# Mixture-of-experts rows: weighted on the way and summed in DRAM by accumulating indirect DMAs

## The reference, cut to what matters

```python
x = x + xattn(layernorm(x), ctx, W_q, W_kv, W_out, ln_gamma, ln_beta)     # x: (2, 512, 128)
x = x + ffn(layernorm(x), Wg, bg, W1, b1, W3, b3, W2, b2)

def ffn(x, ...):                                   # 8 experts, D_MODEL = 128, D_FF = 512
    probs = softmax(x @ Wg + bg)
    top_v, top_i = top_k(probs, 2)
    top_v = top_v / (top_v.sum(-1, keepdims=True) + 1e-6)
    combine = einsum('bsk,bske->bse', top_v, one_hot(top_i, 8))
    out = 0
    for e in range(8):
        h = silu(x @ W1[e] + b1[e]) * (x @ W3[e] + b3[e])
        out = out + combine[..., e:e+1] * (h @ W2[e] + b2[e])
    return out
```

## Time and profile before

| what | value |
|---|---|
| time, median of 3 runs | 189.43 us (188.91 to 189.51) |
| the profiled execution: its own time | 188.9 us |
| the profiled execution: span from first to last instruction | 187.2 us |
| TensorE busy, share of span | 77% |
| VectorE busy | 68% |
| ScalarE busy | 40% |
| GpSimd busy | 42% |
| mean granted TensorE clock | 0.916 of full speed |
| expert loop, first to last scatter | 103.87 to 173.44 us |
| from the landing of the last scatter to the end | 175.68 to 187.2 us |

### The profile page before, as it was taken

One profiled execution on the slowest core, in us unless ns is written; L12 is line 12 of the kernel. 1 busy time (PEld: TensorE's weight loads), 2 busy tenths in 40 slices (PEclk: granted clock), 3 DMA queues, 4 the chain that ended last, 5 costly groups with the idle time before them and its releaser, 6 DMA issues.

```text
span 187.2 us, 3063 instructions
## 1 busy us (share of the span) xinstructions
PE 145.0 (77%) x910; PEld 109.1 (58%) x910; DVE 126.7 (68%) x299; ACT 74.6 (40%) x157; POOL 79.4 (42%) x99
## 2 busy tenths in 40 slices
PE   6597978999999986112399998999999999985000
PEld 6476857899988876111135665676666667664000
DVE  0688999889999378878027676666666666672054
ACT  3176568555666431003013432535344444432000
POOL 2651119553567530100772564565656532324200
PEclk9999999999999999755559999999999999999855
DMA  5999992498000303100121110111111100000272
GB/s 157 321 333 349 349 348 86 210 427 369 7 4 0 112 0 88 30 0 2 42 55 29 32 42 28 42 47 42 42 42 46 44 28 14 32 15 28 61 205 84
DMA packets 16952, 19.62 MB, mean 105 GB/s; under 512 B 1837, under 2 KB 13385, under 8 KB 16681
## 3 DMA queue, kind: packets, MB, share of 16 engines
q1 hardware_dynamic: 14628, 15.54, 24.9%
q0 software_dynamic: 1472, 3.02, 5.4%
q10 hardware_dynamic: 837, 0.87, 1.4%
HBM read 16.28 MB, written 3.15 MB: 104 GB/s over the span
## 4 chain that ended last, share of the span: by engine, by line
PE 56%; DVE 19%; DMA 9%; ACT 7%; issue 5%; POOL 1%; ACTq 1%; DVEq 0%; SPq 0%; POOLq 0%
PE psum L1038 21%; PE psum L1057 9%; PE psum L1089 7%; PE psum L1048 4%; DMA early<-in_L_xattn_W_q_dram 4%; PE psum L1076 3%; DVE perm L726 2%; DVE prob L788 2%; PE psum L836 2%; PE psum L838 2%; PE psum L837 2%; DMA y_back<-y_scratch 2%; ACT probT L523 2%; DVE prob L650 2%; DVE xn L829 2%
## 5 line engine op out<-in xcount | busy, mean ns | idle before, releaser
L1038 PE MATMUL psum<-w,probT 128*128 x92 | 46.0, 623 | 1.0 <-ACT probT L559 1.0
L788 DVE TENSOR_TENSOR prob<-psum,early 128x1024 f32<-128x1024 f32 x23 | 28.2, 1224 | 19.6 <-PE psum L1038 18.5
L446 POOL DMA_INDIRECT y_scratch<-xnT,out_row x23 | 22.6, 982 | 34.2 <-DVE xnT L797 34.2
L438 POOL DMA_INDIRECT g_room<-xf_scratch,idx x23 | 22.4, 973 | 19.2 <-DVE idx L771 12.5
L1057 PEld LDWEIGHTS psum<-w,probT 128*128 128x128 f32 x184 | 22.4, 192 | 10.1 <-issue 10.1
L1057 PE MATMUL psum<-w,probT 128*128 x184 | 24.7, 277 | 2.9 <-ACT probT L574 2.9
L415 POOL TENSOR_TENSOR prob<-prob,rowsum 128x1232 f32<-128x1232 f32 x8 | 18.0, 2249 | 17.4 <-DVE rowsum L641 17.3
L1038 PEld LDWEIGHTS psum<-w,probT 128*128 128x128 f32 x92 | 16.4, 199 | 14.6 <-issue 14.6
L569 ACT ACTIVATE prob<-prob 128x512 f32<-128x512 f32 x23 | 14.5, 629 | 25.5 <-DVE prob L788 25.5
L819 DVE TENSOR_TENSOR probT<-prob 128x512 f32<-128x512 f32 x23 | 15.9, 692 | 11.8 <-ACT prob L569 11.8
L1089 PE MATMUL psum<-vo,probT 128*128 128x128 f32 (+1 forms) x160 | 19.5, 277 | 0.3
(11 more groups left out here) (128 smaller groups left out, 203.8 us busy)
## 6 DMA issues: line engine op xcount, KB each, us to landing
w<-in_L_ffn_W_dram SPq DMA_DIRECT2D x24, 256.0 KB, 5.8
early<-in_L_ffn_b_dram SPq DMA_DIRECT2D x2, 2048.0 KB, 10.5
early<-in_L_xattn_W_kv_dram SPq DMA_DIRECT2D x2, 512.0 KB, 7.2
y_back<-y_scratch SPq DMA_DIRECT2D x4, 256.0 KB, 3.7
early<-in_L_xattn_W_q_dram ACTq DMA_DIRECT2D x1, 512.0 KB, 8.0
early<-in_L_xattn_W_out_dram SPq DMA_DIRECT2D x1, 512.0 KB, 9.8
early<-in_L_ffn_b_dram SPq DMA_DIRECT2D x1, 512.0 KB, 13.8
xf_scratch<-xf SPq DMA_DIRECT2D x2, 256.0 KB, 2.6
```

The lines of the kernel that those rows point to most:

```text
L438: pool.indirect_dma_start(xg[:, j % GR, :], None, xf_dram[:, :], bass.IndirectOffsetOnAxis(ap=idx[:, j:j + 1], axis=0)).then_inc(xg_ok[j % ...
L446: pool.indirect_dma_start(y_dram[:, :], bass.IndirectOffsetOnAxis(ap=out_row[:, j:j + 1], axis=0), y_sb[:, j % YR, :], None).then_inc(y_st ...
L788: dve.tensor_tensor(pre[:, j % 3, :, :], psum[:, 2 * (j % 2):2 * (j % 2) + 2, :], b13[:, :, bass.ds(expert[j], 1), :].rearrange("p a e f - ...
L1038: ins = pe.matmul(psum[:, 2 * (j % 2) + a, :], xt[:, j % 2, :], w13[:, bass.ds(expert[j], 1), a, :].rearrange("p e f -> p (e f)"), start=T ...
```

## The change

Nothing of the sorting or of the matmuls changes. These parts do:

1. **Gates earlier, and through DRAM.** `gates` moves from the expert loop into the routing, after the last `one_hots` and before the instructions that end in `eid` and `idx`. Rows of xf_scratch are 129 elements long (XW): the last is the gate of that (token, k). SP waits for the gates and writes them with two DMAs, each of 1024 elements of 4 B, one for each row. The first gather waits for these too.
2. **Weighting in the loop.** The gathered rows bring their gate along as column 128. h is multiplied by it (a scalar_tensor_tensor in place of a tensor_tensor, 128x512), and so is the bias b2 in `bias_down` (the same exchange of kinds, 128x128).
3. **Sum in DRAM.** SP stores x2 group by group into a new DRAM tensor acc_scratch, right behind the two stores of xf of the group; one more store of zeros fills 128 padding rows. `scatter(j)` adds its rows to acc_scratch by an accumulating indirect DMA. A token's two rows come in different tiles, so each scatter waits until the one before it has landed in whole.
4. **End.** No read back and no sums: when the last scatter has landed, SP and ScalarE each issue one copy of 256 KB from acc_scratch to the output, DRAM to DRAM.
5. **Buffers.** The gather ring gets 23 buffers (one for each tile), the result ring goes from 6 to 4 and waits for the landing of scatter j - 4. `out_row` comes from `idx` by two instructions, behind a wait for it; one iota is gone.

```diff
@@ constants @@
+        XW = P + 1
-        gate_w = sb("gate_w", [P, T, K])
+        gate_w = sb("gate_w", [P, K, T])
-        xf_dram = nc.dram_tensor("xf_scratch", [ROWS, P], F32, kind="Internal")
-        y_dram = nc.dram_tensor("y_scratch", [ROWS + NT * P, P], F32, kind="Internal")
-        GR = 16
-        YR = 6
+        xf_dram = nc.dram_tensor("xf_scratch", [ROWS, XW], F32, kind="Internal")
+        acc_dram = nc.dram_tensor("acc_scratch", [N + P, P], F32, kind="Internal")
+        YR = 4
...
@@ sync @@
             sp.dma_start(xf_dram[PAD_ROW:PAD_ROW + P, :], zero_rows[:, :]).then_inc(xf_st, 16)
+            sp.dma_start(acc_dram[N:N + P, :], zero_rows[:, 0:P]).then_inc(acc_init, 16)
...
                 for k in range(K):
                     row = k * (N + P) + g.start * P
-                    sp.dma_start(xf_dram[row:row + len(g) * P, :].rearrange("(t p) d -> p t d", p=P),
+                    sp.dma_start(xf_dram[row:row + len(g) * P, 0:P].rearrange("(t p) d -> p t d", p=P),
                                  xf[:, g.start:g.stop, :]).then_inc(xf_st, 16)
-
-            for s in range(YR):
-                sp.wait_ge(y_st[s], 16 * len(range(s, NT, YR)))
-            for b in range(B):
+                sp.dma_start(acc_dram[g.start * P:g.stop * P, :].rearrange("(t p) d -> p t d", p=P),
+                             x2[:, g.start:g.stop, :]).then_inc(acc_init, 16)
+            sp.wait_ge(gate_ok, 1)
+            with nc.allow_non_contiguous_dma(reason="one gate for each row"):
                 for k in range(K):
-                    row = k * (N + P) + b * BANK
-                    sp.dma_start(y_back[:, k, b * TB:(b + 1) * TB, :],
-                                 y_dram[row:row + BANK, :].rearrange("(t p) d -> p t d", p=P)).then_inc(back[b], 16)
-            out_v = out.rearrange("b (t p) d -> p (b t) d", p=P)
-            for n, tiles in enumerate(OUT_PARTS):
-                sp.wait_ge(o_ok, tiles.stop)
-                sp.dma_start(out_v[:, tiles, :], xn[:, tiles, :]).then_inc(stored, 16)
-            sp.wait_ge(stored, 16 * len(OUT_PARTS))
+                    row = k * (N + P)
+                    sp.dma_start(xf_dram[row:row + N, P:P + 1].rearrange("(t p) d -> p t d", p=P),
+                                 gate_w[:, k, :].rearrange("p (t o) -> p t o", o=1)).then_inc(xf_st, 16)
+
+            sp.wait_ge(acc_st, 16 * NT)
+            out_v = out.rearrange("b n d -> (b n) d")
+            sp.dma_start(out_v[0:BANK, :], acc_dram[0:BANK, :]).then_inc(stored, 16)
+            sp.wait_ge(stored, 32)
...
@@ gpsimd @@
                 if j == 0:
                     pool.wait_ge(idx_ok, 1)
-                    pool.wait_ge(xf_st, 16 * (1 + K * G))
-                elif j >= GR:
-                    pool.wait_ge(xt_mm, j - GR + 1)
-                pool.indirect_dma_start(xg[:, j % GR, :], None, xf_dram[:, :],
-                                        bass.IndirectOffsetOnAxis(ap=idx[:, j:j + 1], axis=0)).then_inc(xg_ok[j % GR], 16)
+                    pool.wait_ge(xf_st, 16 * (1 + K * G + K))
+                pool.indirect_dma_start(xg[:, j, :], None, xf_dram[:, :],
+                                        bass.IndirectOffsetOnAxis(ap=idx[:, j:j + 1], axis=0)).then_inc(xg_ok[j], 16)
...
                 if j == 0:
                     pool.wait_ge(row_ok, 1)
-                pool.indirect_dma_start(y_dram[:, :], bass.IndirectOffsetOnAxis(ap=out_row[:, j:j + 1], axis=0),
-                                        y_sb[:, j % YR, :], None).then_inc(y_st[j % YR], 16)
+                    pool.wait_ge(acc_init, 16 * (1 + G))
+                else:
+                    pool.wait_ge(acc_st, 16 * j)
+                pool.indirect_dma_start(acc_dram[:, :], bass.IndirectOffsetOnAxis(ap=out_row[:, j:j + 1], axis=0),
+                                        y_sb[:, j % YR, :], None, compute_op=ALU.add).then_inc(acc_st, 16)
...
@@ scalar, behind its loop @@
+            act.wait_ge(acc_st, 16 * NT)
+            act.dma_start(out.rearrange("b n d -> (b n) d")[BANK:N, :], acc_dram[BANK:N, :]).then_inc(stored, 16)
...
@@ vector @@
             one_hots(2)
             one_hots(3)
+            gates()
...
             dve.tensor_scalar(idx[:, :], psum[:, IDX_BANK, 0:NT], row_base[:, 0:1], None, ALU.add).then_inc(idx_ok, 1)
-            link(dve.scalar_tensor_tensor(out=unused[:, :], in0=psum[:, IDX_BANK, 0:NT], scalar=0.0, in1=iota_pad[:, :],
-                                          op0=ALU.is_equal, op1=ALU.mult))
-            dve.scalar_tensor_tensor(out=out_row[:, :], in0=psum[:, IDX_BANK, 0:NT], scalar=row_base[:, 0:1], in1=unused[:, :],
-                                     op0=ALU.add, op1=ALU.add).then_inc(row_ok, 1)
+            dve.wait_ge(idx_ok, 1)
+            link(dve.tensor_scalar(second[:, :], idx[:, :], float(N + P), -float(N + P), ALU.is_ge, ALU.mult))
+            dve.tensor_tensor(out_row[:, :], idx[:, :], second[:, :], ALU.add).then_inc(row_ok, 1)
...
                 if j >= YR:
-                    dve.wait_ge(y_st[j % YR], 16 * (j // YR))
-                dve.tensor_tensor(y_sb[:, j % YR, :], psum[:, 7, 0:P],
-                                  b2[:, bass.ds(expert[j], 1), :].rearrange("p e d -> p (e d)"), ALU.add).then_inc(y_ok, 1)
+                    dve.wait_ge(acc_st, 16 * (j - YR + 1))
+                dve.scalar_tensor_tensor(out=y_sb[:, j % YR, :], in0=b2[:, bass.ds(expert[j], 1), :].rearrange("p e d -> p (e d)"),
+                                         scalar=xg[:, j, P:P + 1], in1=psum[:, 7, 0:P], op0=ALU.mult, op1=ALU.add).then_inc(y_ok, 1)
...
-                    dve.tensor_tensor(h[:, j % 2, :], silu[:, j % 2, :], pre[:, j % 3, 1, :], ALU.mult).then_inc(h_ok, 1)
-                if j == 4:
-                    gates()
-
-            for t in range(T):
-                if t % TB == 0:
-                    dve.wait_ge(back[t // TB], 16 * K)
-                dve.scalar_tensor_tensor(out=x2[:, t, :], in0=y_back[:, 0, t, :], scalar=gate_w[:, t, 0:1], in1=x2[:, t, :],
-                                         op0=ALU.mult, op1=ALU.add).then_inc(half_sum, 1)
-                dve.wait_ge(half_sum, t + 1)
-                dve.scalar_tensor_tensor(out=xn[:, t, :], in0=y_back[:, 1, t, :], scalar=gate_w[:, t, 1:2], in1=x2[:, t, :],
-                                         op0=ALU.mult, op1=ALU.add).then_inc(o_ok, 1)
+                    dve.scalar_tensor_tensor(out=h[:, j % 2, :], in0=silu[:, j % 2, :], scalar=xg[:, j, P:P + 1],
+                                             in1=pre[:, j % 3, 1, :], op0=ALU.mult, op1=ALU.mult).then_inc(h_ok, 1)
```

More of the change, by code:

```diff
@@ L127, in build @@
         count_init = sb("count_init", [P, (T + 1) * E], F16)
-        zero_rows = sb("zero_rows", [P, P])
+        zero_rows = sb("zero_rows", [P, XW])
         lower = sb("lower", [P, E, E])
@@ L147, in build @@
         idx = sb("idx", [P, NT], U32)
-        unused = sb("unused", [P, NT])
+        second = sb("second", [P, NT])
         out_row = sb("out_row", [P, NT], U32)
@@ L174, in build @@
         xt = probT_room[:, 4 * FF:4 * FF + 2 * P].rearrange("p (n d) -> p n d", n=2)
-        xg = g_room[:, 0:GR * P].rearrange("p (n d) -> p n d", n=GR)
+        xg = g_room[:, 0:NT * XW].rearrange("p (n d) -> p n d", n=NT)
         y_sb = xnT[:, 0:YR, :]
@@ L218, in build @@
         xf_st = sem("xf_st")
-        xg_ok = [sem(f"xg_ok{n}") for n in range(GR)]
-        y_st = [sem(f"y_st{n}") for n in range(YR)]
+        xg_ok = [sem(f"xg_ok{n}") for n in range(NT)]
+        acc_st = sem("acc_st")
+        acc_init = sem("acc_init")
+        gate_ok = sem("gate_ok")
         xt_mm = sem("xt_mm")
@@ L232, in build @@
         expo_ok = sem("expo_ok")
-        back = [sem(f"back{n}") for n in range(B)]
-        half_sum = sem("half_sum")
-        o_ok = sem("o_ok")
         stored = sem("stored")
@@ L662, in _ @@
             sums(T - 1)
-            dve.wait_ge(const_ok, 14)
+            dve.wait_ge(const_ok, 13)
             dve.wait_ge(ld["router"], 32)
@@ L727, in one_hots, with gates @@
                                           ALU.is_equal, ALU.mult).then_inc(perm_ok, 1)
+            def gates():
+                dve.wait_ge(expo_ok, 1)
+                link(dve.tensor_reduce(zsum[:, :], expo[:, :, :], AX.X, ALU.add))
+                link(dve.tensor_tensor(den[:, :], expo[:, :, 0], expo[:, :, 1], ALU.add))
+                link(dve.scalar_tensor_tensor(out=den[:, :], in0=zsum[:, :], scalar=1e-6, in1=den[:, :], op0=ALU.mult, op1=ALU.add))
+                link(dve.reciprocal(den[:, :], den[:, :]))
+                dve.tensor_tensor(gate_w[:, :, :], expo[:, :, 0:K].rearrange("p t k -> p k t"),
+                                  den[:, :].rearrange("p (o t) -> p o t", o=1).broadcast_to([P, K, T]), ALU.mult).then_inc(gate_ok, 1)
             late_stats(4)
@@ L795, in bias_down @@
                 if j >= YR:
-                    dve.wait_ge(y_st[j % YR], 16 * (j // YR))
-                dve.tensor_tensor(y_sb[:, j % YR, :], psum[:, 7, 0:P],
```

(18 more changed lines are left out.)

5 lines of the change are left out of this document (removed).

## The result

The changed kernel takes 210.49 us (210.13 to 211.01, 4 runs) against 189.4 us (188.91 to 189.51): the ratio is 1.1115, 95% interval 1.1079 to 1.1152. It is 11% slower, where 1.4% faster was forecast. The profiled execution took 210.13 us, its span is 208.4 us, 21.2 longer than before.

What follows compares the result with a forecast made beforehand. The expert loop was taken as bound by TensorE at 3.158 us a tile. Tail -7.7, stall before gather 0 +4.7 and later last landing +0.4 gave -2.6 us, so 186.8 us against the median; range 183.2 to 197.

Steps and rivals of the forecast that it cites:

- The scatters' spacing: Expert loop: waiting for the previous scatter's landing leaves the period unchanged; the last landing comes 0.4 us later.
- L: Accumulating scatter's time from issue to landing: taken as 2.8 us, between 2.3 and 4.8; free in the loop up to 2.89.
- My lower bound: Least time from issue to landing of an accumulating scatter: the plain scatter's 2.3 us.
- The 0.27: Time in us from a semaphore to GpSimd's next scatter issue, added to the landing time for the spacing.
- A: Rival, expert loop: the accumulating scatters take over from TensorE as the bound; 196.5 us at a 3.3 us landing; chance 0.35.
- its sum: Rival's last landing: 103.87 + 4.7 + 22 x (L + 0.27) + L, for L above 2.89.
- The tail: After the last landing: two DRAM copies replace reads back, sums and stores; 3.85 us for 11.52, 7.7 saved.
- Before gather 0: End of routing: gate DMAs delay gather 0 from 88.51 to 93.2, 4.7 us lost (bounds 2.7 and 8.8).
- the row of 512 B pieces: Gate DMAs before the first gather: each 4 B piece priced like a 512 B store piece, 16.7 ns, adding 2.0 us.
- Rival B: Gate writes before the first gather: 4 B pieces dear at 51 ns, stall 8.8 us, total 190.9 us; chance 0.13.
- The loop's other terms: Expert loop: gates leaving return 1.24 us; two VectorE instructions cost some 0.07 us more each, hidden; no further clock loss.
- The read-modify-write rule: Skill rule on scatters: same-row packets overlap in an engine, against serial row cost; landing 2.5 us, forecast 0.9 lower.

Runs made afterwards that it cites:

- Run 1: Changed kernel with the scatter writing plainly instead of adding, every wait kept: 189.0 us, ratio 0.9961 to the kernel before.
- run 6: Changed kernel with scatters adding only 64 of 128 columns, into a tensor of their own: 207.73 us, ratio 1.0922 to the kernel before.
- Run 5: Changed kernel with a scatter's two waits swapped, first the previous landing, then its own result: 201.63 us, ratio 1.0659 to the kernel before.
- run 7: Kernel before with only the gates moved right behind out_row, into VectorE's idle time: 188.82 us, ratio 0.9944.

## Why the prediction was wrong, step by step

**The step that failed is "The scatters' spacing".** It said that a scatter follows the one before by L + 0.27 with L = 2.8, so 3.07, free under 3.16. It measured 3.92 at the end of the loop and 4.18 on average, and TensorE had to follow. Both terms were too small: L, the time from issue to landing, and the wake, the time from the landing to GpSimd's next issue.

- *L* is 3.17 to 3.3 with nothing else in flight and 3.6 in the median, not 2.8. I placed it by the one part that I thought grew, a read in DRAM. More than half of the growth at the end, 0.58 of 0.93, is GpSimd, whose issue goes from 0.97 to 1.55 and in the loop at times to 2.01. Run 1 shows that the add does it, run 6 that it goes by row and not by byte. My lower bound rested on a plain scatter's issue, which the add doesn't keep.
- *The 0.27* was read from a scatter that has one wait. In the changed scatter the landing is waited for second, behind the result, and from the landing to the issue pass 0.73 to 0.77. Run 5 gets 0.43 of it back by the order of the two, 8.9 us in all, more than the whole gain of the tail; run 1 shows the 0.27 with both waits in place, where the result is what comes last. The sum would have been lost on this term alone: 2.8 + 0.74 = 3.54 is over 3.16.

The rival that came true is A, by its mechanism and its place: the spacing is L plus the wake, GpSimd waits for the landing, and TensorE is no longer full, where before it was busy 50.87 of 50.90 us. Busy time from the first to the last scatter:

```profile
108.77:200.69 91.92, 68.89 (x358) 46.06 (x356) 46.21 (x63) 28.76 (x62) 52.53 (x37) 0.91 0.22 27
```

TensorE has 68.89 of 91.92 us. With the measured spacing and landing its sum gives 103.87 + 4.7 + 22 x 4.18 + 3.17 = 203.7 for the last landing, which came at 203.86. But it carried L alone as the unknown, up to 3.3 in the range, and the wake as known. Had it had 0.74, then L = 3.3 would have been 206.8 us, 22 x 0.47 = 10.3 more than 196.5, and L = 2.8 a loss too. The rest up to 210.5 is mostly the longer landings in the middle of the loop: 22 x (4.18 - 3.3 - 0.74) = 3.1.

**The tail** was right: 7.0 saved for 7.7. The two copies land in 3.3 and 3.9 where 3.3 was taken.

**Before gather 0** was right in sum, 4.82 for 4.7, and that is luck: three errors cancel. The chain there:

```profile
89.01 3.42 DMA xf_scratch<-gate_w
92.43 0.02 issue
92.45 0.02 POOLq L430
92.47 0.86 issue
93.33 2.87 DMA g_room<-xf_scratch,idx
```

The second gate DMA lands in 3.42, so by the landing the 120 further pieces of 4 B cost (3.42 - 2.2) / 120 = 10 ns each and not 16.7, which is 0.78 us less than forecast. The Trainium skill (DMA: Bandwidth & Descriptors, Bandwidth) gives about 10.5 ns as the least for a packet; with its figure the term would have been closer than with the row of 512 B pieces. The engines' own records give less. SP's queue from 88 to 93.3 us, where it carries these two DMAs alone:

```profile
q1 hardware_dynamic: 2080, 0.01, 17.9%
```

That is 0.179 x 16 x 5.3 / 2080 = 7.3 ns a packet, so as a least time the 10.5 isn't borne out here.

Against the 0.78, the second DMA is issued 0.31 later than forecast, and 0.90 us pass from the landing to the gather where I had 0.3. I called that a wait for idx alone, but gather 0 has two waits in both kernels, first for idx and then for the stores. In the kernel before idx came last, 0.29 before the issue; now the stores do, and they are waited for second. It is the same error as in the spacing. Rival B fell with this: small pieces are cheap.

**The loop's other terms** held. No clock was lost on top: gather 0 to scatter 0 takes 15.44 for 15.36. The two kinds of VectorE instruction cost 60 ns more each (L817 752 ns for 692, L804 341 for 282) and nothing of it is on the path: in run 1 the scatters 0 to 6 are 3.158 apart, at (127.92 - 108.97) / 6. The gates' 1.24 us do come back, as run 7 shows on the kernel before; in the changed kernel they came back into a loop that no longer waited for TensorE.

**The read-modify-write rule** of the Trainium skill (same page, Two DMAs through the same engine are not ordered) was taken to speak against a serial cost for the rows. The traces don't contradict it: behind GpSimd's issue an accumulate needs 1.62 us and a plain scatter 1.27. The 0.35 more would be 44 ns for each of the eight rows of an engine if they came one after the other; whether they overlap no run shows. GpSimd's own share is the larger one here, and the prediction had none for it.

## What to carry to other kernels

A wait that makes a stream of DMAs serial turns a latency into a rate: its price is the whole way from issue over landing to the next issue, and it is free only while that is under the period of the loop. Read each of its three terms on a row of the same kind: the issue of the instruction with its new options, and the wake from a wait that stands where the late one will stand. Where there are two waits, try the late one first. And ask whether two in flight would do (two tensors here: 24 us off, of which reading both back takes about 6 again). And before work is moved off an engine look where that engine stands idle: moving five small instructions into VectorE's wait for the first tile gave 0.6%, and sharing the tail between two engines another 0.5%, while the redesign lost 11%.

## What the runs showed of the hardware that I had not expected

- An accumulating indirect DMA of 128 rows makes 112 more packets than a plain one (4048 against 1472 over 23 scatters), and occupies GpSimd for 1.55 us in place of 0.97, for rows of 512 B and of 256 B alike.
- The order of two semaphore waits ahead of an indirect DMA is worth 0.43 to 0.47 us an issue on GpSimd. When the semaphore that comes last is the one waited for second, 0.69 us pass from the separate wait to a scatter (0.86 before gather 0); when it is waited for first, 0.22 to 0.29.
- 4 B pieces written to DRAM with a stride of 516 B take 7.3 ns a packet of an engine's time, and by the landing 10 ns each; by the landing pieces of 512 B took 16.7.
